# A graph layer on one core: the first pair of the product loop as eight block products, with its preparation re-ordered

## The chip, the core and the metric

The kernel runs on one core of a Trainium2 chip. The metric is the device time of one execution in microseconds, the median of the runs shown.

## What is computed

`x` is 64 batches of 128 x 1024 float32; the 1024 columns are the nodes of a graph, the 128 rows are features. Cut to what matters here:

```python
h = relu(layernorm(x))                          # over the 1024 nodes
avg = h.mean(batch)                             # 128 x 1024
xn = avg / norm(avg over features)
sim = (xn.T @ xn + 1) / 2                       # 1024 x 1024
adj = sim + gumbel0 > 1 - sim + gumbel1
mask = clip(adj + adj.T + eye); common = mask @ mask.T
W = adj * where(valid, common**2 / common.max(), 0)
Wn = dinv[:, None] * W * dinv[None, :]          # dinv = column sum ** -0.5
out = x + (adj_w.T @ h[b]) @ Wn + bias          # for each batch b
```

So everything up to `Wn` needs all 64 batches, and the last line is one product with a 1024 x 1024 matrix for each batch.

## The kernel before

**First stage (to about 122 us).** Four trips of 16 batches. SP loads `x` (slots `x1`), VectorE takes the moments (L864, L870), GpSimd turns them into scale and bias in groups of two or four batches (`norms`, L329 to L337), ScalarE does the ReLU (`relu1`, L407) into the slots `h1`. The sum over the batches is shared out: GpSimd adds batches 0, 3, 6, 8, 12 of a trip to `acc` (L345), TensorE adds the rest in PSUM (L646). In the last trip VectorE adds batches 10, 12 and 14 and `acc` to `mine` (L885, L891) and then forms `S` (L895). The Gumbel chunks (eight of 1 MB, L270) are loaded on the same queue, the first four between `x` loads of the last trip (`GUMBEL_AFTER`), and `margin_of(c)` (L876) turns chunk c into one threshold tile. From `S` come the squares (L426), the column norms (L658), `rnorm` (one power on GpSimd, L366), its broadcast (L627) and `xn` (L905). `stay_awake` (L622) is a run of small matmuls with no use of their own; one `n` is two instructions.

**Second stage (to about 190 us).** `sim` by chunks (L671) against `margin` gives `adjm`; `nmask`; then eight chunks e of `common` on TensorE (L760), each with one transposition of `adjm` in its middle (`turn_adj`, L725). VectorE masks each chunk twice (`mask` L952, `mask_t` L961), ScalarE copies the transposed mask (`turned`, L517) and sums its squares (`degree_of`, L523). Between these lie the operands of the first two pairs of batches: `relu2` (L451, L452) makes h in float32 and float16, `h_low` (L936) the float16 remainder, `xw_of` (L742) multiplies by the weights (24 matmuls), `z_of` (L466) evicts, `z_sums` (L371 to L376) forms four sums on GpSimd, `y_high` (L480) and `y_low` (L947) split each into two float16 parts. After the last degree: `bound`, `roots` (L380), `root`, the column maximum (L1011), its transposition (L711), the broadcast of the roots (L780), the top value (`spread`, L715) and the constants from it (L1030 to L1040).

**The matrix.** `rooted` (L1016, eight chunks) scales; `square` (L563) on ScalarE; then the blocks are combined (L1046, L1054, L1059 and L391 on GpSimd) and each combination is split by `high` (L568, ScalarE) and `low` (L1022, VectorE) into `a16`, two float16 parts. `s_alo` counts the finished low parts.

**The product loop.** Batches go in 32 pairs. Each pair is a 2 x 2 block product by seven products instead of eight (combinations of the halves of y times seven combinations of the blocks of A, in `a16[:, :, 0..6]`); a product is 12 matmuls of 512 columns (L789). `pe_pair` interleaves them with `xw_of` of the next pair; `act_pair` evicts partial sums (`partial`, L494) and prepares the next pair; `dve_pair` adds up (L1068 to L1094) and adds `x` (L1083). TensorE's queue and every other are in the order of the code; an engine that waits holds up everything behind it. The waits of the first pair on `s_alo` follow `MADE`. During the first pair TensorE computes no `xw_of` (that of pair 1 is done before); the ReLUs of pair 2 come after it on ScalarE (L593, L594), so `xw_of` of pair 2 lies within pair 1.

Of the kernel before, what the change touches and what calls it, by code (L numbers as in the profile page):

```python
# [30 lines left out]
P = 128  # L31
# [9 lines left out]
GUMBEL_AFTER = (1, 5, 9, 13)  # L41
# [11 lines left out]
def gnn_kernel(nc, x, adj, bias, gumbel, out):  # L53
# [14 lines left out]
    with ExitStack() as ctx:  # L68
# [76 lines left out]
        x_first = {j: obuf[:, j, :] for j in (1, 2, 3)}  # L145
# [8 lines left out]

        ps = ctx.enter_context(nc.psum_tensor("ps", [P, 8, H], F32))
# [14 lines left out]
        ps_xw2 = pair[3]  # L170

# [57 lines left out]
        s_t3 = sem("t3_ready")  # L229
        s_ahi = sem("a_high_ready")  # L230
        s_alo = sem("a_low_ready")
        s_xf = [sem(f"x_first_loaded{j}") for j in (1, 2, 3)]
# [18 lines left out]
        LO, HI = slice(0, H), slice(H, N)  # L251
        GROUPS = ((0, 2), (2, 1), (3, 2), (5, 2))
        MADE = (0, 3, 2, 4, 5, 1, 6)
# [4 lines left out]
        def _(sp):  # L258
# [50 lines left out]
        def _(pool):  # L309
# [68 lines left out]
            def roots(n, a, b):  # L378
# [18 lines left out]
        def _(act):  # L397
# [20 lines left out]
            with act.Fori(0, TRIPS1) as i:  # L418
                for j in range(BODY1):
                    relu1(i, j)  # L420
                    if j in KEEP_AFTER:
                        keep(NK * i + KEEP_AFTER.index(j))

# [8 lines left out]
            def relu2(i, q, b):  # L432
# [8 lines left out]
                if first:  # L441
                    act.wait_ge(s_xf[j - 1], 16)
                else:
                    act.wait_ge(s_x2[j], 16 * (i + 1))
# [9 lines left out]
            def z_of(i, q, b):  # L454
# [11 lines left out]
                nc.scalar.activation(dst, src, ACT.Copy, scale=Y_SCALE / W_SCALE).then_inc(s_z, 1)  # L466

# [29 lines left out]
            def act_pair(i, q, ahead1, ahead2):  # L497
                partial(i, q, 0)
                if ahead1:
                    z_of(i, q + 1, 0)  # L500
# [5 lines left out]
                if ahead1:  # L506
                    z_of(i, q + 1, 1)
# [21 lines left out]
            y_high(0, 0, 0)  # L529
# [4 lines left out]
            y_high(0, 0, 1)  # L534
# [5 lines left out]
            y_high(0, 0, 2)  # L540
            turned(4)
            degree_of(3)
            y_high(0, 0, 3)
            turned(5)
            degree_of(4)
            z_of(0, 1, 0)
            y_high(0, 1, 0)
            turned(6)
            degree_of(5)
            z_of(0, 1, 1)  # L550
            y_high(0, 1, 1)
# [3 lines left out]
            y_high(0, 1, 2)  # L555
            y_high(0, 1, 3)

# [32 lines left out]
            partial(0, 0, 2)  # L590
            act.wait_ge(s_t, 3)
            high(6, spare)
            relu2(0, 2, 0)  # L593
            relu2(0, 2, 1)  # L594
            for q in range(1, PAIRS):
# [8 lines left out]
        def _(pe):  # L604
# [27 lines left out]
            def sums(i, except_for=()):  # L632

                for j in range(BODY1):
                    h = h1[j % HS]
                    if j in KEPT:
                        pe.wait_ge(s_h, BODY1 * i + j + 1)
# [5 lines left out]
                    if j in TENSOR_SUMS and j not in except_for:  # L643
                        pe.wait_ge(s_h, BODY1 * i + j + 1)
# [10 lines left out]
            stay_awake(ps[:, 6, 2 * P:3 * P], 12)  # L655
# [5 lines left out]
            stay_awake(ps[:, 7, 2 * P:3 * P], 7)  # L661
# [87 lines left out]
            for e, c in enumerate(CHUNKS):  # L749
# [33 lines left out]
            spread(1)  # L783
# [10 lines left out]
            def pe_pair(i, q, ahead1, first=False):  # L794
                r = PAIRS * i + q

                def made(mat):
                    if first:
                        pe.wait_ge(s_alo, MADE.index(mat) + 1)

                pe.wait_ge(s_y, 4 * r + 5)
                pe.wait_ge(s_c, 4 * r + 4)
                made(0)
# [17 lines left out]
                made(1)  # L821
# [5 lines left out]
            pe_pair(0, 0, False, True)  # L827
            pe.wait_ge(s_e, C)
            for q in range(1, PAIRS):
# [8 lines left out]
        def _(dve):  # L838
            dve.sem_inc(s_c, 8)
# [38 lines left out]
            margin_of(0)  # L878
            mine = h1[VECTOR_SUMS[0] % HS]
            dve.wait_ge(s_h, B - BODY1 + VECTOR_SUMS[0] + 1)  # L880
            for n, j in enumerate(VECTOR_SUMS[1:]):
                dve.wait_ge(s_h, B - BODY1 + j + 1)
                if n >= 1:
                    dve.wait_ge(s_mine, n)
                nc.vector.tensor_tensor(mine, mine, h1[j % HS], ALU.add).then_inc(s_mine, 1)  # L885
                if n == 0:
                    margin_of(1)
            mine_pool = sum(j in POOL_SUMS for j in VECTOR_SUMS)
            dve.wait_ge(s_mine, len(VECTOR_SUMS) - 1)
# [270 lines left out]
```

## Time and profile before

| | us |
|---|---|
| median of 3 runs (878.41 to 878.64) | 878.57 |
| the profiled execution | 877.09 |
| its span | 875.1 |
| PE busy, 94% | 820.3 |
| DVE busy, 66% | 581.0 |
| ACT busy, 58% | 509.9 |
| POOL busy, 37% | 321.7 |
| mean granted TensorE clock | 0.978 |

The profile calls TensorE PE, its weight loads PEld, VectorE DVE, ScalarE ACT, GpSimd POOL. Times are from the start of the span. Busy time of PE is pipelined and says little by itself; what an engine waited for stands in brackets.

### The profile page before, as it was taken

The numbers are of one execution on the slowest core, as the hardware profiler recorded it, in microseconds if no ns is written. First come the engines' busy times: TensorE is split into PE (matmuls) and PEld (weight loads), VectorE is DVE, ScalarE is ACT, GpSimd is POOL, SyncE is SP. The second block draws the span as 40 slices with busy tenths as digits, with TensorE's granted clock in tenths as the row PEclk, the third lists the DMA queues.
The fourth block names the chain that finished last, engine by engine and source line by source line (L and its number), as shares of the span: only waits on it lengthen the run. The fifth ranks groups of instructions, "written<-read, shape, count | busy, mean of one in ns | idle before, by whom it ended". The sixth has DMA issues, their size and how long they took to land.

```text
span 875.1 us, 13556 instructions
## 1 busy us (share of the span) xinstructions
PE 820.3 (94%) x4740; PEld 427.7 (49%) x4740; DVE 581.0 (66%) x667; ACT 509.9 (58%) x523; POOL 321.7 (37%) x260
## 2 busy tenths in 40 slices
PE   4999899943899999999999999999999999999997
PEld 3544455531454555455545555554555455545553
DVE  7999766869855655666566656555665666566653
ACT  3888804847565665666555645565665666456531
POOL 4788710232033333333343333333333433343320
PEclk9999999976899999999999999999999999999999
DMA  8999802000633222222222223333222222222111
GB/s 348 409 408 396 362 1 73 1 1 0 236 122 113 107 97 97 97 97 96 96 96 96 96 104 135 109 110 111 102 96 96 96 96 96 96 96 97 51 69 74
DMA packets 29545, 111.04 MB, mean 127 GB/s; under 512 B 3408, under 2 KB 3536, under 8 KB 28496
## 3 DMA queue, kind: packets, MB, share of 16 engines
q1 hardware_dynamic: 29520, 110.70, 34.2%
q8 instruction: 16, 0.26, 0.1%
q14 instruction: 9, 0.07, 0.0%
HBM read 77.14 MB, written 33.55 MB: 126 GB/s over the span
## 4 chain that ended last, share of the span: by engine, by line
PE 78%; DVE 8%; issue 6%; POOL 5%; ACT 2%; DMA 0%; POOLq 0%; ACTq 0%; DVEq 0%; SPq 0%
PE ps L789 66%; PE ps L742 8%; DVE stats L864 4%; POOL rstd L335 1%; POOL zbuf L345 1%; PE ps L671 1%; DVE xring L1054 1%; DVE xring L1016 1%; ACT xring L563 0%; ACT zbuf L407 0%; ACT a L568 0%; PE ps L646 0%; PE ps L685 0%; POOL zbuf L374 0%; DVE moments L870 0%
## 5 line engine op out<-in xcount | busy, mean ns | idle before, releaser
L789 PE MATMUL ps<-a,ybuf 128*128 128x512 f16 x2688 | 592.4, 380 | 22.4 <-DVE a L1022 14.8
L789 PEld LDWEIGHTS ps<-a,ybuf 128*128 128x128 f16 x2688 | 261.5, 98 | 329.4 <-issue 19.2
L947 DVE TENSOR_TENSOR ybuf<-zbuf,ybuf 128x1024 f16<-128x1024 f32 (+1 forms) x128 | 168.0, 1312 | 165.9 <-ACT ybuf L480 165.9
L371 POOL TENSOR_TENSOR zbuf<-zbuf 128x512 f32<-128x512 f32 x32 | 40.9, 1277 | 418.1 <-ACT zbuf L466 418.1
L480 ACT ACTIVATE ybuf<-zbuf 128x1024 f16<-128x1024 f32 (+1 forms) x128 | 121.6, 950 | 115.5 <-POOL zbuf L376 102.5
L494 ACT ACTIVATE obuf<-ps,bias_sb,w_out 128x512 f32<-128x512 f32 x64 | 49.4, 772 | 121.6 <-PE ps L789 121.6
L936 DVE TENSOR_TENSOR hring<-hring 128x1024 f16<-128x1024 f32 x56 | 68.6, 1224 | 58.7 <-ACT hring L452 58.7
L742 PEld LDWEIGHTS ps<-w,hring 128*128 128x128 f16 x1344 | 79.7, 98 | 13.4 <-issue 0.4
L742 PE MATMUL ps<-w,hring 128*128 128x128 f16 x1344 | 84.2, 219 | 0.3 <-DVE k L979 0.3
L1083 DVE TENSOR_TENSOR obuf<-obuf,xring 128x1024 f32<-128x1024 f32 x64 | 78.4, 1225 | 2.8
L374 POOL TENSOR_TENSOR zbuf<-zbuf 128x512 f32<-128x512 f32 x32 | 71.7, 2240 | 0.0
L466 ACT ACTIVATE zbuf<-ps 128x1024 f32<-128x1024 f32 x56 | 57.3, 1022 | 21.6 <-PE ps L742 21.4
L376 POOL TENSOR_TENSOR zbuf<-zbuf 128x512 f32<-128x512 f32 x32 | 69.1, 2158 | 0.0
L451 ACT ACTIVATE hring<-xring,nbias,rstd 128x1024 f32<-128x1024 f32 x53 | 65.1, 1228 | 3.7 <-issue 3.7
L452 ACT ACTIVATE hring<-xring,nbias,rstd 128x1024 f16<-128x1024 f32 x53 | 65.1, 1228 | 0.0
L373 POOL TENSOR_TENSOR zbuf<-zbuf 128x512 f32<-128x512 f32 x32 | 50.6, 1582 | 2.5
L864 DVE BATCH_NORM_STATS2 stats<-xring 128x6 f32<-128x512 f32 x64 | 38.9, 671 | 0.7 <-issue 0.7
L864 DVE BATCH_NORM_STATS2 stats<-ybuf 128x6 f32<-128x512 f32 x56 | 34.2, 669 | 2.7 <-DMA ybuf<-in_x_dram 2.7
L646 PE MATMUL ps<-hring,ident 128*128 128x512 f32 x76 | 34.0, 593 | 0.0
L494 ACT ACTIVATE p<-ps,bias_sb,w_out 128x512 f32<-128x512 f32 x32 | 24.7, 773 | 11.4 <-PE ps L789 11.4
L1088 DVE SCALAR_TENSOR_TENSOR obuf<-ps,w_out,obuf 128x512 f32<-128x512 f32 x32 | 24.0, 750 | 10.2 <-PE ps L789 10.1
L646 PE MATMUL ps<-zbuf,ident 128*128 128x512 f32 x60 | 28.2, 603 | 2.5 <-ACT zbuf L407 2.4
(125 smaller groups left out, 629.3 us busy)
## 6 DMA issues: line engine op xcount, KB each, us to landing
xring<-in_x_dram SPq DMA_DIRECT2D x96, 512.0 KB, 4.5
out_dram<-obuf SPq DMA_DIRECT2D x64, 512.0 KB, 2.9
ybuf<-in_x_dram SPq DMA_DIRECT2D x28, 512.0 KB, 9.8
a<-in_L_gnn_gumbel_dram SPq DMA_DIRECT2D x7, 1024.0 KB, 14.4
obuf<-in_x_dram SPq DMA_DIRECT2D x7, 512.0 KB, 5.9
obuf<-in_L_gnn_gumbel_dram SPq DMA_DIRECT2D x1, 1024.0 KB, 22.6
w<-in_adj_dram SPq DMA_DIRECT2D x1, 64.0 KB, 1.8
bias_sb<-in_L_gnn_bias_dram SPq DMA_DIRECT2D x1, 0.5 KB, 2.1
```

The lines of the kernel that those rows point to most:

```text
L374: nc.gpsimd.tensor_tensor(z[:, 6, :], z[:, 1, :], z[:, 0, :], ALU.subtract).then_inc(s_zs, 1)
L376: nc.gpsimd.tensor_tensor(z[:, 7, :], z[:, 2, :], z[:, 5, :], ALU.subtract).then_inc(s_zs, 1)
L451: nc.scalar.activation(h32, src, ACT.Relu, bias=bias, scale=scale).then_inc(s_h32, 1)
L452: nc.scalar.activation(h16[b][:, 0, :], src, ACT.Relu, bias=bias, scale=scale).then_inc(s_hhi, 1)
L480: nc.scalar.activation(y16[:, q % 2, 0, a:a + n, :], z[:, a + 1:a + 1 + n, :], ACT.Copy).then_inc(s_yhi, 1)
L494: nc.scalar.activation(dst, src, ACT.Identity, bias=bias_sb[:, 0:1], scale=w_out[:, 0:1]).then_inc(s_v, 1)
L742: mm = nc.tensor.matmul(ps_xw2[:, c * P:(c + 1) * P], h16[b][:, hk, c * P:(c + 1) * P], w16[:, wk, :], start=(hk == wk == 0), stop=(hk == ...
L789: mm = nc.tensor.matmul(bank[q % 2], y16[:, q % 2, yk, u, c * P:(c + 1) * P], a16[:, ak, mat, c, :], start=(start and c == yk == ak == 0), ...
L864: nc.vector.bn_stats(stats[:, j % 4, 6 * m:6 * m + 6], x1[j][:, m * H:(m + 1) * H]).then_inc(s_bn, 1)
L936: nc.vector.tensor_tensor(h16[b][:, 1, :], h32, h16[b][:, 0, :], ALU.subtract).then_inc(s_hlo, 1)
L947: nc.vector.tensor_tensor(y16[:, q % 2, 1, a:a + n, :], z[:, a + 1:a + 1 + n, :], y16[:, q % 2, 0, a:a + n, :], ALU.subtract).then_inc(s_y, 1)
L1083: nc.vector.tensor_tensor(ob, ob, xring[:, j, :], ALU.add).then_inc(s_out, 1)
```

## The change

- **First pair.** `first_pair` computes pair 0 as eight block products with the four blocks themselves: blocks 0, `A12` (kept in slot 6), 1, 2, for both batches: 96 matmuls for 84. Its four results are evicted straight by ScalarE (`FIRST_OUT`). `z_sums(0)` falls away; `y_high_first` and `y_low_first` make four 512-column parts. The combinations (`SECOND`) are made for pair 1, and slot 6 gets its own when the first four products are done.
- **Order.** `low` of 0, `A12`, 1, 2 come first. The third combination moves from GpSimd (L391) to VectorE. ReLUs, `xw_of` and `z_of` of pair 2, and the ReLUs of pair 3, come before or within the making of the matrix; `xw_of(0,1,1)` moves from behind chunk 6 to behind chunk 4; `spread(1)` comes ahead of the broadcast of the roots, and 14 `stay_awake` ahead of `turn(1)`. Seven batches instead of three are loaded through `obuf` (`x_first`).
- **First stage.** All Gumbel chunks are loaded behind the last `x`. VectorE does the ReLUs of batches 10, 12 and 14 of the last trip itself, two instructions each; all five early margins lie behind `S`.

```diff
@@ SyncE @@
-                if j in GUMBEL_AFTER:
-                    load_gumbel(GUMBEL_AFTER.index(j))
-            for c in range(len(GUMBEL_AFTER), C):
+            for c in range(C):
                 load_gumbel(c)
...
@@ GpSimd @@
-            z_sums(0)
+            pool.sem_inc(s_zs, 4)
+            z_sums(1)
             roots(0, 0, 6)
-            z_sums(1)
             roots(1, 6, C)
-            pool.wait_ge(s_a32, C)
-            pool.wait_ge(s_t, 1)
-            nc.gpsimd.tensor_tensor(rows_hi[:, :, HI], rows_lo[:, :, HI], rows_hi[:, :, HI],
-                                    ALU.subtract).then_inc(s_t3, 1)
...
@@ ScalarE, from the last degrees on @@
             degree_of(7)
-            y_high(0, 1, 2)
             y_high(0, 1, 3)
+            relu2(0, 2, 0)
+            relu2(0, 2, 1)
...
             for c in range(HC):
                 square(rows_hi, 0, c)
+            z_of(0, 2, 0)
             act.wait_ge(s_a32, HC)
             high(0, rows_hi[:, :, LO])
-            square(rows_lo, 1, 0)
-            square(rows_lo, 1, 1)
+            act.wait_ge(s_e, C)
+            high(A12, rows_hi[:, :, HI])
+            for c in range(HC):
+                square(rows_lo, 1, c)
+            z_of(0, 2, 1)
+            act.wait_ge(s_a32, C)
+            high(1, rows_lo[:, :, LO])
+            high(2, rows_lo[:, :, HI])
...
+            act.wait_ge(s_t, 3)
             high(5, rows_hi[:, :, HI])
+            relu2(0, 3, 0)
+            act.wait_ge(s_t, 4)
+            act.wait_ge(s_mm, 14 + 3)
+            high(6, spare)
             act.wait_ge(s_wout, 1)
+            act.wait_ge(s_hhi, 6)
+            for n, (b, m, bank) in enumerate(FIRST_OUT):
+                act.wait_ge(s_mm, 14 + 4 + n)
+                nc.scalar.activation(o[0][b][:, m], bank, ACT.Identity, bias=bias_sb[:, 0:1],
+                                     scale=w_out[:, 0:1]).then_inc(s_first, 1)
+            relu2(0, 3, 1)
+            act.wait_ge(s_hhi, 7)
+            act_pair(0, 1, True, False, False)
...
@@ TensorE @@
-            stay_awake(ps[:, 6, 2 * P:3 * P], 12)
+            stay_awake(ps[:, 6, 2 * P:3 * P], 7)
...
-                if e == 6:
+                if e == 4:
                     xw_of(0, 1, 1)
             pe.wait_ge(s_m, C)
+            stay_awake(ps[:, 3, 0:P], 14)
             turn(1)
+            spread(1)
...
-            spread(1)
+            xw_of(0, 2, 0)
+            xw_of(0, 2, 1)
...
+            def first_pair():
+                pe.wait_ge(s_y, 8)
+                for k, mat in enumerate(FIRST):
+                    pe.wait_ge(s_alo, k + 1)
+                    for b in (0, 1):
+                        u = ((0, 3), (1, 2))[k // 2][b]
+                        bank = FIRST_OUT[2 * (k % 2) + b][2]
+                        for c in range(HC):
+                            for yk, ak in ((0, 0), (0, 1), (1, 0)):
...
@@ VectorE, first stage @@
-            margin_of(0)
...
+                nc.vector.tensor_scalar(x1[j], x1[j], rstd[:, t:t + 1], nbias[:, t:t + 1], ALU.mult,
+                                        ALU.add).then_inc(s_mine, 1)
...
+                    nc.vector.scalar_tensor_tensor(out=mine, in0=x1[j], scalar=0.0, in1=mine, op0=ALU.max,
+                                                   op1=ALU.add).then_inc(s_mine, 1)
...
+            margin_of(0)
+            margin_of(1)
             dve.wait_ge(s_n2, 1)
             nc.vector.tensor_scalar(norm2[:], ps_norm, NORM_MIN ** 2, None, ALU.max).then_inc(s_n2s, 1)
             margin_of(2)
             margin_of(3)
             margin_of(4)
...
@@ VectorE, the matrix @@
+            h_low(0, 2, 0)
+            dve.wait_ge(s_qrow, 2)
+            for c in range(HC):
+                rooted(rows_hi, 0, c)
+            for c in range(HC):
+                rooted(rows_lo, 1, c)
+            h_low(0, 2, 1)
+            low(0, 0, rows_hi[:, :, LO])
+            low(1, A12, rows_hi[:, :, HI])
...
+            low(2, 1, rows_lo[:, :, LO])
+            low(3, 2, rows_lo[:, :, HI])
...
+            nc.vector.tensor_tensor(rows_hi[:, :, HI], rows_lo[:, :, HI], rows_hi[:, :, HI],
+                                    ALU.subtract).then_inc(s_t, 1)
+            low(4, 3, spare)
...
+            low(5, 4, rows_hi[:, :, LO])
+            low(6, 5, rows_hi[:, :, HI])
+            h_low(0, 3, 0)
+            low(7, 6, spare)
...
+            add_x(0, 0, 0)
             add_x(0, 0, 1)
-            for q in range(1, PAIRS):
+            h_low(0, 3, 1)
+            dve_pair(0, 1, True, False)
+            for q in range(2, PAIRS):
                 dve_pair(0, q, True, True)
```

## Rows read from the trace of the kernel before

**Rows 1.** The chain that ended last: start us, us, what.

```profile
209.53 6.62 DVE xring L1054
...
222.40 17.04 PE ps L789 x72
...
247.29 12.95 PE ps L789 x60
260.25 1.34 PE ps L742 x24
```

**Rows 2.** Stretches of 1 us: PE, PEld, DVE, ACT, POOL, PE's granted clock, DMA.

```profile
109.00:110.00 1.00, 1.00 (x2) 0.49 (x3) 1.00 (x1) 0.74 (x1) 0.00 (x0) 0.53 0.00 0
...
184.00:185.00 1.00, 0.00 (x0) 0.00 (x0) 1.00 (x2) 0.91 (x1) 1.00 (x1) 0.58 0.00 0
...
211.00:212.00 1.00, 1.00 (x5) 0.41 (x4) 1.00 (x1) 0.00 (x0) 1.00 (x1) 0.77 0.00 0
```

**Rows 3.** VectorE by time, end of the first stage: start, us, what [idle before].

```profile
99.97 3.18 DVE L876 TENSOR_TENSOR a<-a 128x1024 f32<-128x1024 f32 x1
...
112.65 1.29 DVE L895 TENSOR_TENSOR hring<-ps,hring 128x512 f32<-128x512 f32 x2 [2.42 <-PE ps L646]
...
121.01 0.69 DVE L905 SCALAR_TENSOR_TENSOR hring<-hring,ps 128x512 f32<-128x512 f32 x1 [2.74 <-PE ps L627]
```

**Rows 4.** GpSimd by time, the same stretch.

```profile
99.69 2.37 POOL L345 TENSOR_TENSOR zbuf<-zbuf,hring 128x1024 f32<-128x1024 f32 x1
102.02 1.18 POOL L329 TENSOR_TENSOR var_eps<-moments,eps 128x2 f32<-128x2 f32 x1
...
106.05 0.20 POOL L337 TENSOR_TENSOR nbias<-neg_mean,rstd 128x2 f32<-128x2 f32 x1
117.28 2.48 POOL L366 TENSOR_TENSOR rnorm<-norm,neg_half 128x8 f32<-128x8 f32 x1 [11.03 <-DVE norm L899]
```

**Rows 5.** TensorE by time, the same stretch.

```profile
103.98 1.88 PE L646 MATMUL ps<-zbuf,ident 128*128 128x512 f32 x4
108.89 3.65 PE L646 MATMUL ps<-obuf,ident 128*128 128x512 f32 x4 [3.03 <-ACT obuf L407]
112.33 2.91 PE L622 MATMUL ps<-ones,zeros 128*128 128x128 f32 x24
```

**Rows 6.** All engines by time, 160 to 250 us.

```profile
166.46 3.62 PE L760 MATMUL ps<-xring 128*128 128x512 bf16 x16
...
167.71 1.05 ACT L523 ACTIVATE a<-a 128x1024 f32<-128x1024 f16 x1
...
181.43 1.22 DVE L961 SCALAR_TENSOR_TENSOR a<-ps,a 128x1024 f16<-128x1024 f32 x1 [1.60 <-PE ps L760]
...
188.63 3.62 PE L780 MATMUL ps<-ident,qf 128*128 128x128 f32 x16
...
192.28 1.28 DVE L1016 SCALAR_TENSOR_TENSOR xring<-a,qf,ps 128x1024 f32<-128x1024 f16 x1 [2.00 <-PE ps L780]
...
207.55 7.25 PE L789 MATMUL ps<-a,ybuf 128*128 128x512 f16 x24 [14.80 <-DVE a L1022]
```

**Rows 7.** Groups by line and form: busy, mean ns of one, idle before.

```profile
L936 DVE TENSOR_TENSOR hring<-hring 128x1024 f16<-128x1024 f32 x56 | 68.6, 1224 | 58.7 <-ACT hring L452 58.7
L451 ACT ACTIVATE hring<-xring,nbias,rstd 128x1024 f32<-128x1024 f32 x53 | 65.1, 1228 | 3.7 <-issue 3.7
...
L371 POOL TENSOR_TENSOR zbuf<-zbuf 128x512 f32<-128x512 f32 x32 | 40.9, 1277 | 418.1 <-ACT zbuf L466 418.1
...
L864 DVE BATCH_NORM_STATS2 stats<-ybuf 128x6 f32<-128x512 f32 x56 | 34.2, 669 | 2.7 <-DMA ybuf<-in_x_dram 2.7
...
L1022 DVE TENSOR_TENSOR a<-xring,a 128x2048 f16<-128x2048 f32 x5 | 11.2, 2279 | 0.0
...
L568 ACT ACTIVATE a<-xring 128x2048 f16<-128x2048 f32 x5 | 9.3, 1903 | 5.9 <-DVE xring L1054 5.8
...
L563 ACT ACTIVATE xring<-xring,kappa 128x1024 f32<-128x1024 f32 x8 | 8.6, 1134 | 8.3 <-DVE kappa L1037 8.3
```

More of the change, by code:

```diff
@@ L144, in gnn_kernel @@
         spare = hring[:, 3:5, :].rearrange("p a (b n) -> p (a b) n", b=2)
-        x_first = {j: obuf[:, j, :] for j in (1, 2, 3)}
+        x_first = {j: obuf[:, j % 4, :] for j in range(1, BODY)}
         z = zbuf[:, :, :].rearrange("p a (b n) -> p (a b) n", b=2)
@@ L228, in gnn_kernel @@
         s_t = sem("t_ready")
-        s_t3 = sem("t3_ready")
         s_ahi = sem("a_high_ready")
         s_alo = sem("a_low_ready")
-        s_xf = [sem(f"x_first_loaded{j}") for j in (1, 2, 3)]
+        s_xf = {j: sem(f"x_first_loaded{j}") for j in range(1, BODY)}
+        s_first = sem("first_pair_block_read")
         s_h32 = sem("h32_ready")
@@ L417, in _, with relus @@
             act.sem_inc(s_xw1used, 1)
-            with act.Fori(0, TRIPS1) as i:
+            act.sem_inc(s_v, 3)
+            def relus(i, except_for=()):
                 for j in range(BODY1):
-                    relu1(i, j)
+                    if j not in except_for:
+                        relu1(i, j)
                     if j in KEEP_AFTER:
                         keep(NK * i + KEEP_AFTER.index(j))
+            with act.Fori(0, TRIPS1 - 1) as i:
+                relus(i)
+            relus(TRIPS1 - 1, VECTOR_SUMS)
             for half, m in enumerate((LO, HI)):
@@ L506, in act_pair @@
                 if ahead1:
-                    z_of(i, q + 1, 1)
+                    if evict:
+                        z_of(i, q + 1, 1)
                     y_high(i, q + 1, 1)
@@ L528, in _ @@
             turned(0)
-            y_high(0, 0, 0)
+            y_high_first(0)
             turned(1)
@@ L533, in _ @@
             z_of(0, 0, 1)
[L534 removed]
+            y_high_first(1)
             turned(2)
@@ L635, in sums @@
                     h = h1[j % HS]
+                    skipped = sum(v < j for v in except_for)
                     if j in KEPT:
-                        pe.wait_ge(s_h, BODY1 * i + j + 1)
+                        pe.wait_ge(s_h, BODY1 * i + j + 1 - skipped)
                         pe.wait_ge(s_xw1used, NK * i + KEPT.index(j) + 1)
@@ L660, in _ @@
             mm.then_inc(s_n2, 1)
-            stay_awake(ps[:, 7, 2 * P:3 * P], 7)
+            stay_awake(ps[:, 7, 2 * P:3 * P], 11)
             pe.wait_ge(s_rn, 1)
@@ L792, in product, with pe_pair @@
                 mm.then_inc(s_mm, 1)
-            def pe_pair(i, q, ahead1, first=False):
+            def first_pair():
[7 more added lines that the diff above has]
+                            for yk, ak in ((0, 0), (0, 1), (1, 0)):
+                                mm = nc.tensor.matmul(bank, y16[:, 0, yk, u, c * P:(c + 1) * P],
+                                                      a16[:, ak, mat, c, :], start=(k < 2 and c == yk == ak == 0),
+                                                      stop=(k >= 2 and c == HC - 1 and yk == 1), skip_group_check=True)
+                        if k + b > 0:
+                            mm.then_inc(s_mm, 1)
+            def pe_pair(i, q, ahead1, second=False):
                 r = PAIRS * i + q
                 def made(mat):
-                    if first:
-                        pe.wait_ge(s_alo, MADE.index(mat) + 1)
+                    if second and mat in SECOND:
+                        pe.wait_ge(s_alo, 5 + SECOND.index(mat))
                 pe.wait_ge(s_y, 4 * r + 5)
                 pe.wait_ge(s_c, 4 * r + 4)
-                made(0)
                 product(q, 0, 0, ps_b, True)
@@ L820, in pe_pair @@
                 product(q, 5, 5, ps_b, False)
-                made(1)
+                if second:
+                    pe.wait_ge(s_first, 4)
                 product(q, 1, 1, ps_a, True)
@@ L825, in pe_pair @@
                 product(q, 2, 6, ps_b, False)
-            pe_pair(0, 0, False, True)
+            first_pair()
             pe.wait_ge(s_e, C)
-            for q in range(1, PAIRS):
+            pe_pair(0, 1, False, True)
+            for q in range(2, PAIRS):
                 pe_pair(0, q, True)
@@ L984, in _ @@
             mask(1)
-            y_low(0, 0, 0)
+            y_low_first(0)
             mask_t(1)
@@ L989, in _ @@
             mask_t(2)
-            y_low(0, 0, 1)
+            y_low_first(1)
             mask(3)
@@ L1005, in _ @@
             mask(7)
+            y_low(0, 1, 2)
             root(0, 0, 6)
-            y_low(0, 1, 1)
             bound(1, 6, C)
@@ L1115, in dve_pair @@
                 add_x(i, q, 1)
-            upper0(0, 0)
-            low(6, spare)
-            upper1(0, 0)
-            y_low(0, 1, 3)
-            h_low(0, 2, 0)
-            lower0(0, 0)
             add_x(0, 0, 0)
-            h_low(0, 2, 1)
-            lower1(0, 0)
             add_x(0, 0, 1)
-            for q in range(1, PAIRS):
+            h_low(0, 3, 1)
+            dve_pair(0, 1, True, False)
+            for q in range(2, PAIRS):
                 dve_pair(0, q, True, True)
```

132 lines of the change are left out of this document (59 added, 73 removed).

## The prediction

> **What bounds the kernel now.** I read the chain of waits first. From 222.40 us on it is TensorE's products without a gap: 72 matmuls in 17.04 us and then the steady loop, 0.216 us for a matmul of 512 columns (12.95 for 60) and 1.34 for one `xw_of` [rows 1]. So a microsecond won ahead of the third pair is won at the end. The loop after that is the same work in both kernels; I cost it at nothing. Pair 1 starts at 236.85 (the 12 matmuls, 2.59 us, ahead of the first `xw_of`, which starts 17.04 after 222.40). Pair 2 starts 2.59 us before the chain's next `xw_of` at 260.25, at 257.66 [rows 1].
>
> Ahead of the loop three stretches matter. The timeline of all engines shows the first product at 207.55 [rows 6], so pair 0 takes 29.3 us for 84 matmuls that need 18.1: 11.2 us are waits, because the combinations are late. One of them, 2048 elements on VectorE, takes 6.62 us [rows 1] where the same form elsewhere takes 2.28 [rows 7]: it stands behind GpSimd. Before that, the second stage is TensorE without a gap (16 matmuls in 3.62 us [rows 6]) until VectorE waits 1.60 us for its last chunk at 181.43 [rows 6]. At the end of the first stage GpSimd forms the last scale behind its own addition, and each of its small operations waits for a VectorE one: started at 102.02, done at 106.25, the first of them 1.18 us for two elements a partition [rows 4].
>
> The clock: TensorE is granted half (1.2 of 2.4 GHz) at 109, at 184 and until 211 us [rows 2]. Four sums take 3.65 us after an idle of 3.03, and 1.88 before it [rows 5]; the first products take 7.25 us for 24 where 5.18 would do [rows 6].
>
> **The change, part by part.** All times stay on the clock of the profile before.
>
> *Gumbel behind x.* VectorE waits 2.7 us for x in the first stage [rows 7]. They go, so its moments end at 97.3 and not 100.0 [rows 3]. The transfers themselves are covered: the first margin is now read after 111 us, and eight chunks that used to be read from 100 us on have 10 us more. But the last scale is GpSimd's, behind its addition at 99.69 to 102.06 [rows 4], and that isn't earlier.
>
> *ReLUs on VectorE.* What was one addition of 1.2 us a batch becomes two operations. No row shows a float32 tensor_scalar of 1024 in SBUF; the bounds are nothing and the 1.22 us of the other 1024-element forms [rows 7]. With 1.22: the two operations of batch 10 push back GpSimd's scale of batches 12 and 13 by about 1.2; that of batch 12 goes ahead of GpSimd's addition, 1.2 more (102.1 to 104.5); then ReLU-and-add and the addition of `acc`, 1.2 each, fall between GpSimd's last small operations, which end at 108.3. ScalarE's ReLU of batch 15 takes 1.23 and ends at 109.6; TensorE, idle since 105.86, is at half clock again: 3.65, so `S` at 113.3. With nothing: scale at 106.0, ReLU done at 107.3, full clock, 1.88: 109.2. I take the middle, 111.3, against 112.65 [rows 3]. If VectorE and GpSimd never met, TensorE's own queue would set it: 105.86 plus 1.88, 107.7 to 108.1.
>
> The Trainium skill speaks against this part. GPSIMD Engine Reference, section 1, says that GpSimd shares its SBUF interfaces with VectorE and collides with its two-port modes and its two-input operations; VectorE: DVE Perf Modes, "Mode 2×_2P", has a float32 tensor_scalar in that mode, at twice the pace. By it these would last some 0.6 us, an estimate, and `S` come near 111. The rows agree on the collision.
>
> *From `S` to `xn`.* Before 8.36 us [rows 3]. Fewer `stay_awake` (12 are 2.91 us [rows 5]) let the norms be there at `S` + 3.1, but VectorE has two margins first: 1.29 + 2.35, norm at + 3.8. GpSimd's power 2.48 [rows 4], then 1.25 for the broadcast: + 7.6. Three margins follow the norm; if the power holds VectorE up, the last ends 1.1 later. I take 8.2. `xn` at 119.5 against 121.01: front gain 1.5. Ends: 113.3 + 8.8 (1.1 lost) and 108.1 + 7.6 (5.3 won). From here on I leave the front gain aside and add it at the end.
>
> *The middle.* `xw_of(0,1,1)` now stands behind chunk 4 (done at 168.3, half way in the 16 matmuls at 166.46 [rows 6]). It needs `z_of(0,1,0)`, which stands on ScalarE behind `degree_of(3)`: 167.71 + 1.15, two shorter casts at 0.6 in front of it instead of one at 1.05, so 169.0, and evicted at 170.0. TensorE stands 2.0 us, and the last chunk comes 2.0 later. Behind it GpSimd's sums of pair 1 no longer stand ahead of the last root (they are done by then), which gives back 1.9, but a `y_low` of 1.2 stands between mask and root: in all +0.75 at the column maximum. `stay_awake` 14 is 28 x 0.12 = 3.4 us behind the last mask and just ends before that; the idle ahead of it is 2.5 us, shorter than the 3.0 us after which the clock was half, so the roots' broadcast is made in 2.0 and not 3.62 [rows 6]. Then the top value, `y_low` and `h_low` come first on VectorE: `rooted` starts at 193.0 against 192.28 [rows 6].
>
> *To the first product.* Eight `rooted` at 1.2, `h_low` 1.15 and one `low` of 2.28 [rows 7]: 206.0. ScalarE (its four squares wait behind a ReLU pair until 195.5; 4 x 1.13, one eviction, cast 1.90 [rows 7]: 202.5) is in time. TensorE has `xw_of(0,2,1)` first, at half clock, 203.8 to 206.4. First product 206.4, 1.15 earlier.
>
> *Pair 0.* 96 matmuls: 20.7 at full clock, and 0.7 more, as the 2.6 us of `xw_of` have used most of the slow start. Blocks 3 and 4 are in time: the low part of block 1 is there at 214 (ScalarE until 211.7, VectorE 2.28), wanted at 217.5. End 227.85: 21.4 us instead of 29.3, 7.9 won.
>
> *Pair 1.* Its two `xw_of` are gone (2.7 us): 18.13. But its third product needs `partial(0,1,0)`, and on ScalarE that stands behind `relu2(0,3,1)`, which waits for `h_low(0,3,0)`, which VectorE has behind three combinations and five `low`: from 214 on seven operations of 2.28 less overlap and 1.2: 230. GpSimd's sums of pair 2, 4 x 1.28 [rows 7], start at 209.5 and take VectorE's turn for some 2: 231.9. Two ReLUs 2.3, partial 0.77: 235.0, where TensorE is there at 232.8. Stall 2.2. Pair 1 takes 20.3 for 20.8. Pair 2 starts at 248.2 instead of 257.66: 9.5 won. New loads of x have from 226 and 231 us and are wanted at 234 and later; SP waits for nothing earlier.
>
> Sum: 1.5 + 9.5 = 11.0. The profiled execution is 877.09 and the median 878.57, so 866.1 in its frame and **867.6** for the median. A measurement of this kernel tells 0.2% (1.8 us) from no change.
>
> **The rivals.** *Front gain in full:* GpSimd slips between VectorE's operations, TensorE is not interrupted. For it: VectorE now has waits between its operations. Against it: a margin and an addition met at 99.7 and the margin took 3.18 us instead of 1.2 [rows 3, 4]. 5.3 + 9.5: 863.8. *The products start early but the rest is late:* clock half at the roots' broadcast (+1.6), the front as at its worse end (-1.1), three us more of stall in pair 1 because every `low` meets a GpSimd sum: 9.5 - 1.6 - 1.1 - 3.0 = 3.8: 874.8. *The eight products don't run as a block:* the low part of block 1 needs a cast behind four squares, two casts and an eviction on ScalarE, and 3.5 us of slack is all; late by 3 it costs 3, inside the range above. *Slower than before:* the wait of pair 1's third product. It costs one for one from the moment when `h_low(0,3,0)` ends after 229.7, and outweighs all the rest beyond 231.9 + 11 = 243. That is so if the operations of VectorE that stand ahead of it are held as the one at 209.53 was, 4.3 us each for three of them [rows 1]: 13 us on top of the forecast, 880.6. Against it: GpSimd's operations there are of 1.28 us [rows 7], 5.1 in all, and can't hold more than they last.
>
> **How the numbers follow.** Forecast 0.52, front in full 0.2, late rest 0.2, slower 0.05, no change 0.03. The range leaves out the last two and the outer half of each of the middle ones: 862.5 to 874.0. Own range of the forecast: 864.5 to 870.5. Faster 0.92, same 0.03, slower 0.05.
>
> **What would show it.** `S` at 111.3 (if under 109, the first rival); moments done near 97.3; GpSimd's last `nbias` between 106 and 108.3; TensorE idle about 2 us between chunks 4 and 5; granted clock full at the roots' broadcast; 96 matmuls of the first pair without a wait, in about 21.4 us; one wait of TensorE for a partial sum in pair 1, 2 us; from pair 2 to the end 617.4 us as before. A longer wait there, or a wait between the four block groups, makes the prediction wrong in the middle; any difference in the loop makes its ground wrong.

## The result and the profile after

The changed kernel takes 867.40 us (median of 4 runs, 867.18 to 868.64) where the kernel before took 878.49 beside it. The ratio is 0.9888 with a 95% interval of 0.9873 to 0.9903: 1.1% faster. The prediction was 867.6.

| | before | after |
|---|---|---|
| profiled execution, us | 877.09 | 867.24 |
| its span, us | 875.1 | 865.5 |
| PE busy, us | 820.3 | 825.9 |
| DVE / ACT / POOL busy, us | 581.0 / 509.9 / 321.7 | 582.5 / 507.1 / 314.8 |
| mean granted TensorE clock | 0.978 | 0.988 |

The chain that ended last in the changed kernel (start, us, what), to set beside [rows 1]:

```profile
105.88 1.25 ACT obuf L403
107.17 2.00 PE ps L665 x4
...
229.97 1.23 ACT hring L454
231.23 0.79 ACT obuf L501
232.06 18.60 PE ps L811 x72
250.66 1.34 PE ps L761 x24
```

The chain no longer goes through the combinations just ahead of the loop but through one ReLU and one partial sum in pair 1 (L454, L501). Behind them 72 matmuls take 18.60 us where the steady loop needs 15.55. Pair 2 starts 2.59 us ahead of the `xw_of` at 250.66, at 248.07 instead of 257.66: 9.6 us earlier, which is the whole difference of the spans (875.1 less 865.5). The loop behind it is unchanged, as the prediction had it: 617.4 us from the start of pair 2 to the end in both (865.5 less 248.07, 875.1 less 257.66).

The end of the first stage, VectorE by time in the changed kernel:

```profile
97.00 1.70 DVE L926 TENSOR_SCALAR ybuf<-ybuf,rstd,nbias 128x1024 f32<-128x1024 f32 x1
98.73 0.71 DVE L930 TENSOR_SCALAR hring<-ybuf 128x1024 f32<-128x1024 f32 x1
100.31 2.95 DVE L926 TENSOR_SCALAR ybuf<-ybuf,rstd,nbias 128x1024 f32<-128x1024 f32 x1 [0.86 <-POOL nbias L337]
...
109.26 1.29 DVE L937 TENSOR_TENSOR hring<-ps,hring 128x512 f32<-128x512 f32 x2 [1.31 <-PE ps L665]
...
112.81 3.50 DVE L915 TENSOR_TENSOR a<-a 128x1024 f32<-128x1024 f32 x3
116.77 0.69 DVE L949 SCALAR_TENSOR_TENSOR hring<-hring,ps 128x512 f32<-128x512 f32 x1 [0.47 <-PE ps L645]
```

The same stretch on GpSimd:

```profile
102.66 0.64 POOL L329 TENSOR_TENSOR var_eps<-moments,eps 128x2 f32<-128x2 f32 x1
...
105.17 0.67 POOL L337 TENSOR_TENSOR nbias<-neg_mean,rstd 128x2 f32<-128x2 f32 x1
113.04 2.48 POOL L366 TENSOR_TENSOR rnorm<-norm,neg_half 128x8 f32<-128x8 f32 x1 [7.20 <-DVE norm L941]
```

and on TensorE:

```profile
107.17 1.98 PE L665 MATMUL ps<-obuf,ident 128*128 128x512 f32 x4 [1.42 <-ACT obuf L403]
```

The moments end at 97.0, `S` starts at 109.26 (before 112.65 [rows 3]), `xn` at 116.77 (before 121.01). The last scale is complete at 105.84 instead of 106.25 [rows 4], only 0.4 us earlier; ScalarE then has one ReLU to do and not two, and the four sums take 1.98 us and not 3.65 [rows 5]. The tensor_scalar of a ReLU with scale and bias takes 2.95 us where GpSimd's addition is in its way (100.31) and 0.81 where it isn't (at 105.88, a row not shown); the maximum alone takes 0.71 (98.73).

From the last chunks to pair 1, all engines by time:

```profile
165.61 1.50 PE L761 MATMUL ps<-w,hring 128*128 128x128 f16 x24 [1.53 <-ACT zbuf L468]
...
178.93 1.21 DVE L1010 SCALAR_TENSOR_TENSOR a<-ps,a 128x1024 f16<-128x1024 f32 x1
...
185.50 2.05 PE L801 MATMUL ps<-ident,qf 128*128 128x128 f32 x16
...
188.02 9.61 DVE L1066 SCALAR_TENSOR_TENSOR xring<-a,qf,ps 128x1024 f32<-128x1024 f16 x8
...
201.36 22.10 PE L826 MATMUL ps<-a,ybuf 128*128 128x512 f16 x96
...
211.97 3.35 DVE L1103 TENSOR_TENSOR xring<-xring,hring 128x2048 f32<-128x2048 f32 x1
213.13 3.32 POOL L376 TENSOR_TENSOR zbuf<-zbuf 128x512 f32<-128x512 f32 x1
...
223.30 5.34 PE L811 MATMUL ps<-a,ybuf 128*128 128x512 f16 x24
...
228.82 1.24 ACT L453 ACTIVATE hring<-obuf,nbias,rstd 128x1024 f32<-128x1024 f32 x1 [1.01 <-issue]
...
232.06 18.60 PE L811 MATMUL ps<-a,ybuf 128*128 128x512 f16 x72 [3.42 <-ACT obuf L501]
```

TensorE waits 1.53 us for an eviction ahead of `xw_of(0,1,1)` at 165.61, the roots' broadcast takes 2.05 and not 3.62 [rows 6], the eight products start at 201.36 and end without a wait at 223.30. Then come two products of pair 1, and 3.42 us of waiting for a partial sum. VectorE's combination takes 3.35 us, where one of 2048 elements takes 2.28 [rows 7], and GpSimd's sum beside it 3.32 for 1.28 [rows 7]: each waits for the other. What the clock did around that wait (the columns are those of [rows 2]):

```profile
230.00:231.00 1.00, 0.00 (x0) 0.00 (x0) 1.00 (x2) 1.00 (x2) 0.00 (x0) 1.00 0.80 266
231.00:232.00 1.00, 0.00 (x0) 0.00 (x0) 1.00 (x2) 0.97 (x3) 0.00 (x0) 0.56 1.02 385
...
236.00:237.00 1.00, 1.00 (x4) 0.33 (x3) 0.00 (x0) 0.00 (x0) 0.00 (x0) 0.50 1.01 414
237.00:238.00 1.00, 1.00 (x4) 0.32 (x3) 0.00 (x0) 0.60 (x1) 0.00 (x0) 0.53 1.05 430
```

The mean of 0.56 in the second of these puts the fall at about 231.1, 2.5 us after TensorE's last matmul (228.64) and 0.9 before work came; the clock was half until about 237.9. So four differences make up the 9.6 us, against the prediction's:

| stretch | predicted, us won | measured |
|---|---|---|
| to `xn` | 1.5 | 4.24 |
| `xn` to the first product | 1.15 | 1.95 |
| pair 0 | 7.9 (21.4 for 29.3) | 7.36 (21.94) |
| pair 1 | 0.5 (20.3 for 20.8) | -3.96 (24.77) |
| sum | 11.0 | 9.59 |

The sum was good because errors had opposite signs: the front was better than forecast by 2.7 us, pair 1 worse by 4.5. Even so the sum is 1.4 us short; the prediction had 866.1 for the profiled execution, which took 867.24. Its 867.6 for the median came out because the profiled execution of the kernel before lay 1.5 us below its median, and that of the changed kernel only 0.2. The runs below are about the front, the middle and pair 1. None of them undoes the eight block products alone: that pair 0's 7.36 us are theirs and the re-ordered preparation's rests on the two traces, and how they divide is open.

### The profile page after: what moved, and what is told of

It is laid out like the page before. It is cut to its first block, busy times and chain, and to the rows that moved or that the text cites. A ratio compares the mean times of both kernels' runs of the same rounds, so it can differ in the third digit from the quotient of the medians.

```text
span 865.5 us, 13587 instructions
## 1 busy us (share of the span) xinstructions
PE 825.9 (95%) x4771; PEld 431.2 (50%) x4778; DVE 582.5 (67%) x669; ACT 507.1 (59%) x522; POOL 314.8 (36%) x255
## 4 chain that ended last, share of the span: by engine, by line
PE 77%; DVE 10%; issue 4%; ACT 4%; POOL 3%; DMA 0%; POOLq 0%; DVEq 0%; ACTq 0%; SPq 0%
PE ps L811 65%; PE ps L761 8%; DVE stats L903 4%; PE ps L779 1%; POOL rstd L335 1%; DVE a L1072 1%; DVE xring L1066 1%; POOL zbuf L345 1%; PE ps L690 1%; ACT zbuf L403 0%; ACT xring L574 0%; ACT a L579 0%; PE ps L704 0%; DVE moments L909 0%; ACT hring L454 0%
## 5 line engine op out<-in xcount | busy, mean ns | idle before, releaser
L811 PE MATMUL ps<-a,ybuf 128*128 128x512 f16 x2604 | 573.6, 380 | 3.4 <-ACT obuf L501 3.4
L811 PEld LDWEIGHTS ps<-a,ybuf 128*128 128x128 f16 x2604 | 253.2, 98 | 301.1 <-ACT obuf L501 3.9
L991 DVE TENSOR_TENSOR ybuf<-zbuf,ybuf 128x1024 f16<-128x1024 f32 x124 | 163.9, 1321 | 165.7 <-ACT ybuf L487 165.7
L487 ACT ACTIVATE ybuf<-zbuf 128x1024 f16<-128x1024 f32 x124 | 117.6, 950 | 110.4 <-POOL zbuf L376 97.2
L501 ACT ACTIVATE obuf<-ps,bias_sb,w_out 128x512 f32<-128x512 f32 x62 | 47.9, 773 | 126.6 <-PE ps L811 126.6
L453 ACT ACTIVATE hring<-xring,nbias,rstd 128x1024 f32<-128x1024 f32 x49 | 60.2, 1228 | 0.0
L454 ACT ACTIVATE hring<-xring,nbias,rstd 128x1024 f16<-128x1024 f32 x49 | 60.1, 1227 | 0.0
L501 ACT ACTIVATE p<-ps,bias_sb,w_out 128x512 f32<-128x512 f32 x31 | 24.0, 774 | 10.9 <-PE ps L811 10.9
```

What stands on the lines that cost most here:

```text
L453: nc.scalar.activation(h32, src, ACT.Relu, bias=bias, scale=scale).then_inc(s_h32, 1)
L487: nc.scalar.activation(y16[:, q % 2, 0, a:a + n, :], z[:, a + 1:a + 1 + n, :], ACT.Copy).then_inc(s_yhi, 1)
L501: nc.scalar.activation(dst, src, ACT.Identity, bias=bias_sb[:, 0:1], scale=w_out[:, 0:1]).then_inc(s_v, 1)
L811: mm = nc.tensor.matmul(bank[q % 2], y16[:, q % 2, yk, u, c * P:(c + 1) * P], a16[:, ak, mat, c, :], start=(start and c == yk == ak == 0), ...
L991: nc.vector.tensor_tensor(y16[:, q % 2, 1, a:a + n, :], z[:, a + 1:a + 1 + n, :], y16[:, q % 2, 0, a:a + n, :], ALU.subtract).then_inc(s_y, 1)
```

## The experiments

All are edits of the changed kernel unless said otherwise. They ran in three groups (the front; the wait in pair 1 and the second stage; together), each on one chip with the kernel before beside it; the ratio is to that one. The changed kernel itself ran only in the first group, so in the other two a difference to its 867.40 us is one between chips, where the kernel before had medians of 877.07, 878.12 and 877.23. Executions of one kernel differ by 1.5 us and more (the kernel before: 875.23 to 879.10 in the first group); one reason is in the traces below. Where a stretch is disputed I read it in the trace.

### The front, taken apart

**The changed kernel again.**

> The changed kernel once more, as the base for the others of this call: ratio near 0.989, S at about 109.3 us, 24 + 72 matmuls of pair 1 with a wait of 3.4 us between them.

867.40 us, ratio 0.9888 (0.9872 to 0.9905); `S` at 109.14, wait 3.60.

**The whole front of before.**

```diff
+GUMBEL_AFTER = (1, 5, 9, 13)     # four chunks between the last x
-            relus(TRIPS1 - 1, VECTOR_SUMS)
+            relus(TRIPS1 - 1)
...
+            margin_of(0)             # VectorE adds, and makes margins early, as before
             mine = h1[VECTOR_SUMS[0] % HS]
```

> The changed kernel with the first stage of before (Gumbel chunks between the last x, ReLUs on ScalarE, margins early, stay_awake 12 and 7). Theory: the front is worth what the profiles show, 4.2 us up to xn, and nothing of it is lost later, so xn is back at 121.0 and the time is 4.2 us above the changed kernel, 871.6. Rival (the front's gain is partly given back in waits later, so that undoing it costs less): under 870.

867.95 us, ratio 0.9896 (0.9878 to 0.9914): only 0.55 above the changed kernel beside it. The theory's 4.2 fell, and the rival's number came out. TensorE at the end of the first stage in this kernel:

```profile
108.48 1.98 PE L668 MATMUL ps<-obuf,ident 128*128 128x512 f32 x4 [2.85 <-ACT obuf L406]
110.31 2.84 PE L643 MATMUL ps<-ones,zeros 128*128 128x128 f32 x24
```

`S` came at 110.58 and not at 112.65, though the code of the front is that of before and TensorE had idled 2.85 us: this time the clock was full, and the sum of the last batch took 1.98 us instead of 3.65 [rows 5]. So some 2 us of the 3.4 that the two first profiles show at `S` are the clock in one execution. `xn` is at 118.90, 2.25 after the base's 116.65. Of these 2.25 only 1.0 are left at the start of pair 2 (248.61 for 247.62): the 72 matmuls behind the wait in pair 1 (3.18 us here, 3.60 in the base) took 17.16 us here, 18.43 in the base.

**Only the transfers' order as before.**

```diff
                 load1(TRIPS1 - 1, j)
+                if j in GUMBEL_AFTER:
+                    load_gumbel(GUMBEL_AFTER.index(j))
```

> The changed kernel with four Gumbel chunks between the last x as before; ReLUs stay on VectorE. Theory: VectorE's moments end at 100 and not 97.3, and as VectorE now has five operations after them, S comes 2 to 3 us later; time 2.5 us above the changed kernel. Rival (GpSimd's scales set the end of the stage, so the transfers' order is worth nothing): within 0.5 us.

865.21 us, ratio 0.9858 (0.9841 to 0.9874): faster than the changed kernel's 867.40, which neither side expected. VectorE and GpSimd by time:

```profile
99.90 2.50 DVE L929 TENSOR_SCALAR ybuf<-ybuf,rstd,nbias 128x1024 f32<-128x1024 f32 x1
...
108.60 1.29 DVE L940 TENSOR_TENSOR hring<-ps,hring 128x512 f32<-128x512 f32 x2 [0.23 <-PE ps L668]
```

```profile
98.00 0.20 POOL L332 TENSOR_TENSOR var_eps<-moments,eps 128x2 f32<-128x2 f32 x1
...
102.68 1.22 POOL L338 TENSOR_TENSOR rstd<-var_eps,neg_half 128x2 f32<-128x2 f32 x1
103.98 1.20 POOL L340 TENSOR_TENSOR nbias<-neg_mean,rstd 128x2 f32<-128x2 f32 x1
```

The moments do come at 99.9, but then VectorE's first operations no longer fall on the scales of batches 12 and 13 (0.20 us for the first small operation instead of 0.64 in the changed kernel), and `S` is at 108.60, 0.5 earlier. Loading Gumbel behind x is worth nothing here: VectorE's 2.7 us of waiting for x were not on the path. Another 1.3 us of the lead are in the clock after the wait of pair 1 (17.17 us for 72 where the base has 18.43). The profiled execution, at 866.78 the longest of the four, gave most of both back: 14 `stay_awake` took 5.02 us for 3.39, and the products started 1.1 later than the base's. The combination of this order with the edits below was not run.

**ReLUs back on ScalarE,** Gumbel and margins as in the changed kernel.

```diff
-                nc.vector.tensor_scalar(x1[j], x1[j], rstd[:, t:t + 1], nbias[:, t:t + 1], ALU.mult,
-                                        ALU.add).then_inc(s_mine, 1)
...
+                nc.vector.tensor_tensor(mine, mine, h1[j % HS], ALU.add).then_inc(s_mine, 1)
```

> The changed kernel with the ReLUs of batches 10, 12 and 14 of the last trip back on ScalarE, VectorE only adding; Gumbel behind x and all margins behind S stay. Theory (the ReLUs on VectorE are what brought S forward): ScalarE has two ReLUs after the last scale instead of one, S at 111 to 112, time 2 us above. Rival (what brought it forward is only that no margin stands in GpSimd's way): the last scale ends at about 104.5, S at 109.5, time within 0.5 us.

867.60 us, ratio 0.9882 (0.9865 to 0.9899), and in the trace:

```profile
101.78 0.20 POOL L329 TENSOR_TENSOR var_eps<-moments,eps 128x2 f32<-128x2 f32 x1
...
102.98 0.72 POOL L337 TENSOR_TENSOR nbias<-neg_mean,rstd 128x2 f32<-128x2 f32 x1
```

```profile
108.26 1.29 DVE L931 TENSOR_TENSOR hring<-ps,hring 128x512 f32<-128x512 f32 x2 [0.76 <-PE ps L665]
```

The last scale is there at 103.70, 2.1 us before the changed kernel's, and `S` at 108.26, 0.9 before. The rival holds, and the ReLUs on VectorE cost about 0.9. What helps is that the margins went from between the sums to behind `S`. No run moves the margins alone, but the trace of the kernel with the whole front of before, whose ReLUs are on ScalarE too, bears it out: GpSimd starts its last scale at the same 101.78 there, though that kernel has the old order of transfers, and with a margin of VectorE beside its first operations (100.29 to 102.92, the next from 103.98) it is done at 106.03 and not at 103.70. These 2.3 us are the whole difference of the two `S` (110.58 and 108.26). The 0.9 don't show in the time, because in this execution TensorE's `stay_awake` of 14 fell to half clock: 4.79 us instead of 3.39, and with it the roots came 1.4 us later.

### The wait in pair 1

**TensorE kept busy in the wait.**

```diff
+                if second:
+                    stay_awake(ps[:, 6, 0:P], 12)
                 pe.wait_ge(s_v, 3 * r + 1)
```

> The changed kernel with 24 small matmuls (12 stay_awake) on TensorE ahead of the wait for the first partial sum in pair 1. They take about 2.9 us, less than the wait. Theory: TensorE goes on at full clock after the wait, the 72 matmuls behind it take 15.6 us and not 18.6, the wait's end is unmoved; time 3.0 us below the changed kernel. Rival (the 72 are slow for want of operands): 18.6 stays, no gain.

865.84 us, ratio 0.9866 (0.9849 to 0.9884).

```profile
232.03 15.71 PE L811 MATMUL ps<-a,ybuf 128*128 128x512 f16 x72 [0.45 <-ACT obuf L501]
```

The products start again at 232.03, as before the edit (232.06), and 72 of them take 15.71 us. The operands were there; it was the clock. Span 862.6 against 865.5, the predicted 3 us in the profiled execution. In the medians it is only 1.6: the profiled execution is the fastest of its five, the others are 1.4 to 1.6 us above it, and no trace shows where they lost that.

**Two partial sums ahead of the ReLUs.**

```diff
+            partial(0, 1, 0)
+            partial(0, 1, 1)
             relu2(0, 3, 1)
             act.wait_ge(s_hhi, 7)
-            act_pair(0, 1, True, False, False)
+            y_high(0, 2, 0)
+            partial(0, 1, 2)
+            for g in (1, 2, 3):
+                y_high(0, 2, g)
```

> The changed kernel with the first two partial sums of pair 1 ahead of the last ReLU pair on ScalarE. Theory: the wait of 3.4 us for a partial sum goes, and with it the half clock: pair 1 takes 18.2 to 19.5 us instead of 24.8, time 5.5 us below the changed kernel. Rival (the wait moves to the third partial sum or to y of pair 2): gain under 3 us.

862.33 us, ratio 0.9823 (0.9803 to 0.9842): 5.1 below the changed kernel, where 5.5 were expected.

```profile
222.96 21.19 PE L816 MATMUL ps<-a,ybuf 128*128 128x512 f16 x96
```

96 matmuls without a wait (84 of pair 1 and 12 of pair 2). Neither the third partial sum nor y of pair 2 became a wait. Pair 2 starts at 241.40 in this trace and at 247.62 in the base's, 6.2 us earlier, which is the wait and the clock behind it. So the whole pair-1 term is the place of one ReLU pair on ScalarE.

**GpSimd's sums held back.**

```diff
+            pool.wait_ge(s_t, 4)
             with pool.Fori(2, TRIPS * PAIRS) as r:
                 z_sums(r)
```

> The changed kernel with GpSimd's four sums for pair 2 held until VectorE has made the last combination. Theory: the two combinations take 2.28 us instead of 3.35 and the two low parts before them gain 1.1 together, so h_low(0,3,0) ends 3.2 us sooner, the wait in pair 1 is under 0.5 us and the clock stays full: 6 us below the changed kernel. Rival (VectorE is not held by GpSimd, the operations are just that long): no gain, or a loss where y of pair 2 comes late.

866.41 us, ratio 0.9873 (0.9855 to 0.9891): about 1 below the changed kernel, not 6.

```profile
210.81 2.29 DVE L1104 TENSOR_TENSOR xring<-xring,hring 128x2048 f32<-128x2048 f32 x1
213.01 2.28 DVE L1105 TENSOR_TENSOR xring<-xring 128x2048 f32<-128x2048 f32 x1
...
225.30 2.28 DVE L981 TENSOR_TENSOR hring<-hring 128x1024 f16<-128x1024 f32 x1
...
230.91 17.40 PE L812 MATMUL ps<-a,ybuf 128*128 128x512 f16 x72 [2.15 <-ACT obuf L502]
```

Both combinations are 2.28 us long now: GpSimd had been holding them. But the held sums then fell on the next low parts and on `h_low` (2.28 us for 1.22), so `h_low(0,3,0)` ended 1.2 us sooner and not 3.2, the wait was still 2.15 us, and the clock still fell: the granted clock is half from 231.5 to 234.8, and the 72 matmuls took 17.40 us for 15.55. A wait of 2.15 us is about the 2.2 that the prediction put here. Neither side's number; the mechanism is the theory's, but moving a conflict is not removing it.

### The second stage

**`xw_of(0,1,1)` behind chunk 5.**

```diff
-                if e == 4:
+                if e == 5:
                     xw_of(0, 1, 1)
```

> The changed kernel with xw_of(0,1,1) behind chunk 5 instead of 4. Theory: TensorE's wait of 1.5 us for the eviction goes and the last chunk comes 1.5 us sooner, all of it won at the end: 1.5 us below. Rival (something else sets the root): GpSimd's sums of pair 1 start 3 us later and stand ahead of the roots again: no gain or a loss.

866.96 us, ratio 0.9876 (0.9857 to 0.9895).

```profile
179.45 3.39 PE L640 MATMUL ps<-ones,zeros 128*128 128x128 f32 x28 [2.45 <-DVE a L1001]
182.68 0.27 PE L730 MATMUL ps<-ident,col 128*1 128x128 f32 x1
```

The wait of 1.53 us is gone, the column maximum is at 181.83 instead of 183.6, and the eight products start 1.8 us sooner (199.49), so what was to be shown is shown in the trace. The times don't show it: the median is 0.4 us below the changed kernel's. The profiled execution took 863.83 us, 1.8 of its lead from here and 1.4 from the clock behind the wait of pair 1 (17.07 us for 72); the other four are at 865.66 to 867.07, with a mean clock of 0.986 to 0.990 against its 0.991, and have no trace. The trace also shows `turn(1)` at 182.68, 0.7 after the maximum is done. That is so in the changed kernel too (maximum done at 183.87, `turn(1)` at 184.55): even at full clock 14 `stay_awake` are too long and hold the roots by 0.7.

### Together

**The partial sums first, again,** as the base of the last group:

> The kernel of e5 once more (the first two partial sums of pair 1 ahead of the last ReLU pair), as the base of this call: no wait in pair 1, about 862.3 us.

861.00 us, ratio 0.9816 (0.9799 to 0.9834). Its trace has 96 matmuls of pairs 1 and 2 without a wait, in 21.09 us.

**The same with the front of before:**

> The kernel of e5 with the first stage of before. With the wait of pair 1 in place, going back to the front of before cost 2.2 us up to xn and only 0.5 us at the end. Theory (the rest was given back by the clock after that wait, which ran 17.1 us for 72 matmuls instead of 18.6): without the wait the whole 2.2 us show at the end, time 2.2 us above e5's kernel. Rival (the front's gain is lost elsewhere): again 0.5 us.

866.11 us, ratio 0.9859 (0.9835 to 0.9883), 5.1 above the base. TensorE by time:

```profile
186.48 4.95 PE L648 MATMUL ps<-ones,zeros 128*128 128x128 f32 x28 [2.50 <-DVE a L1004]
```

```profile
108.52 3.78 PE L673 MATMUL ps<-obuf,ident 128*128 128x512 f32 x4 [2.84 <-ACT obuf L406]
```

In this execution the clock was half at the last sum (3.78 us after an idle of 2.84), and again at `stay_awake`. `xn` came at 121.94, 5.2 after the base's 116.75, and the span is 6.7 longer: 5.2, and 1.5 for `stay_awake`. One of its four executions took 863.07 us, 2.1 above the base's median, which is what a full clock in the front would give; it has no trace. So, without the wait in pair 1, all that the front loses arrives at the end. By the traces the front is worth 2.2 us at full clock (the run of the whole front of before, above) and 5.2 at half; the theory had only the first of these.

**Three edits together** (ReLUs on ScalarE, `xw_of` behind chunk 5, partial sums first):

> The changed kernel with three edits: ReLUs of the last trip back on ScalarE (S at 108.3), xw_of(0,1,1) behind chunk 5, the two partial sums ahead of the ReLUs. Theory: 0.9 + 1.75 + the gain of e5, 859.7 us. Rival (stay_awake of 14 runs at half clock, or past the column maximum, and holds the roots): 1 to 2 us more.

859.65 us, ratio 0.9790 (0.9772 to 0.9808). The five executions fall in two groups, 858.12 and 858.35, and 859.65 to 860.25. The profiled one is of the second, with `stay_awake` at 5.02 us. So the expected 859.7 came out by luck: it was reckoned from 862.3 for the partial sums first, which took 861.00 here, so the two other edits brought 1.35 us of their 2.65. The rest is the rival's half clock: in the trace `turn(1)` stands 2.3 us behind the finished maximum (183.63 for 181.32) and not 0.7.

**And `stay_awake` spread over the idle stretch:**

```diff
+            pe.wait_ge(s_z, 4)
+            stay_awake(ps[:, 6, 0:P], 10)
             pe.wait_ge(s_m, C)
-            stay_awake(ps[:, 3, 0:P], 14)
+            stay_awake(ps[:, 3, 0:P], 9)
```

> The kernel before it, with 10 stay_awake in TensorE's 2.5 us ahead of the last mask, and 9 instead of 14 behind it. Theory: the clock is full at every execution from the last chunk to the broadcast of the roots, which starts right behind the column maximum: 0.6 us below the kernel before it, and 1.7 us below in executions where that one fell to half clock; spread of its runs smaller. Rival (the clock falls all the same): no difference.

857.68 us, ratio 0.9774 (0.9758 to 0.9791), all five executions from 857.57 to 857.79.

```profile
178.87 2.27 PE L645 MATMUL ps<-ones,zeros 128*128 128x128 f32 x18 [0.21 <-DVE a L1002]
181.47 0.27 PE L735 MATMUL ps<-ident,col 128*1 128x128 f32 x1 [0.33 <-DVE col L1062]
...
225.46 15.71 PE L818 MATMUL ps<-a,ybuf 128*128 128x512 f16 x72 [0.41 <-ACT obuf L501]
```

The idle ahead of the last mask is 0.21 us instead of 2.45, `turn(1)` comes right behind the maximum, and the spread of the executions is gone. This is the best version: 9.7 us below the changed kernel's median and 2.3% below the kernel before beside it.

## Why the prediction was right, and where it wasn't

*Pair 0.* Right: 21.94 us for a predicted 21.4, no wait between the four blocks, and the start at half clock behind `xw_of(0,2,1)` as worked out (198.83 to 201.36 at 2.74 us for 24).

*What takes the time before.* The prediction calls all 11.2 us of pair 0 waits. 7.59 of them are one wait, for a partial sum that ScalarE has behind the casts of the combinations:

```profile
222.40 17.04 PE L789 MATMUL ps<-a,ybuf 128*128 128x512 f16 x72 [7.59 <-ACT obuf L494]
```

The other 3.6 are half clock: 24 matmuls in 7.25 us for 5.18, and these 72 in 17.04 for 15.55. The forecast for pair 0 doesn't hang on this division.

*To `xn`.* The step that failed is "I take the middle, 111.3". `S` came at 109.26, which is 2.0 of the 2.7 us by which this stretch was off. Three terms were too dear. The tensor_scalar was bounded by 1.22 us and takes 0.71 to 0.81 alone; the estimate of 0.6 that the prediction gave beside it, from the Trainium skill (VectorE: DVE Perf Modes, "Mode 2×_2P"), was nearer than the row of another form. The sum of batch 15 was reckoned between the two clocks and ran at full. And behind `S` the power doesn't hold VectorE (113.04 to 115.52 on GpSimd): the three margins beside it and behind took 3.50 us in all, the last ended at 116.31, before the broadcast was there. The reading of what limits this stage was right: GpSimd's scale, not the transfers. The collision of VectorE's ReLUs with GpSimd was rightly foreseen and costs 0.9 us (the run with the ReLUs on ScalarE); what the prediction did not see is that the margins, moved out of GpSimd's way by the same change, more than pay for it.

*The middle.* The wait for the eviction was 1.53 us for 2.0, and the column maximum came 0.2 us earlier relative to `xn` instead of 0.75 later (the three terms given for it, 2.0 - 1.9 + 1.2, make 1.3 and not 0.75). `stay_awake` did not end just before the maximum but 0.7 us behind it. The clock held, as reckoned from an idle of 2.5 us. In three of the edited kernels it was half behind the same gap (28 small matmuls in 5.02, 4.79 and 4.95 us for 3.39: the old transfer order, the ReLUs on ScalarE, and the front of before with the partial sums first), so this step was right for this one by luck.

*Pair 1.* The step that failed is "Stall 2.2". The place and the chain were right: `partial(0,1,0)` behind `relu2(0,3,1)` behind `h_low(0,3,0)` behind VectorE's queue. GpSimd's four sums held VectorE by 1.07 us three times, 3.2 in all, where I took 2, and the wait became 3.42. What was missing altogether is what a wait of that length does: the clock fell, and cost 3.05 us more over the next 72 matmuls. These two, 1.2 and 3.05, are all but 0.2 of the 4.5 us that pair 1 was worse than forecast. The rows to see it by were there: [rows 2] and [rows 5] show a fall after 3.0 us of idleness, and the row above, the same 72 matmuls behind a wait, is in [rows 1] with its 17.04 us. I compared only the 2.5 us of the other gap with the 3.0, and not this one, which the sum put 0.8 us short of it. It would not have been safe there either: with the sums held back the wait was 2.15 us, and the fall cost 1.85.

*The rivals.* "Front gain in full" came nearly true in its stretch (4.24 us of 5.3) and "the rest is late" in its own, and beyond (pair 1 4.5 us worse than forecast, where that case had 3.0): both at once, which none of the cases was.

## What to carry to other kernels

When work is moved earlier on one engine's queue, look for the first instruction behind it that the critical engine waits for: here one ReLU pair ahead of a 0.8 us eviction cost 5 us. Count a wait of TensorE of 2 to 4 us twice, once for itself and once for the clock after it: here the clock cost 1.5 to 3.05 us more behind each such wait in pair 1. Treat gaps of 2.5 us as a source of spread too: with pair 1 mended, filling the one ahead of the last mask (and shortening the `stay_awake` behind it) took the executions from 2.1 us apart to 0.2. And when a change has several parts in one stretch, undo them one by one; the part with the plausible story (ReLUs on the idle engine, transfers re-ordered) was not the one that paid.

## What the runs showed of the hardware that I had not expected

The same idle gap leads to different clocks in different executions of the same code: after 2.85 us of idleness the last sum took 1.98 us in one kernel, after 2.84 us 3.78 in another with the same front. The clock can fall behind as little as 2.15 us of waiting, and then only 0.5 us after the work has started again (231.4 for 230.91, the sums held back). What a fall costs differs too: 72 matmuls took 17.1 to 17.2 us behind waits of 3.17, 3.18 and 3.26 us, and 18.4 to 18.6 behind 3.42, 3.60 and 3.65. The first three were at half clock for another 2.6 to 3.0 us after the products had started again, the others for 5.3 to 5.9. And the durations of GpSimd and VectorE side by side fit turns by whole instructions: a GpSimd operation of 1.28 us beside 2048-element operations of VectorE takes 3.3, and adds 1.07 to the VectorE one.
